# A two-layer decoder on one core: row of maxima ahead of maxima and values projection, stacked reciprocal parts, separate bank rings in the first attention

## What is computed

```python
# first attention: 16 heads of 8 numbers, softmax over 512 keys
dots = jnp.einsum('bhid,bhjd->bhij', q, k) * scale
attn = jax.nn.softmax(dots, axis=-1)
out = jnp.einsum('bhij,bhjd->bhid', attn, v)
# second attention: 16 heads of 64 numbers, queries from the 512 tokens,
# keys and values from 154 context rows and the same 512 tokens (666 keys)
w = jnp.einsum('bhqd,bhkd->bhqk', q * scale, k * scale)
w = jax.nn.softmax(w.astype(jnp.float32), axis=-1).astype(q.dtype)
out = jnp.einsum('bhqk,bhkd->bhqd', w, v)
return out.transpose(0, 2, 1, 3).reshape(B, S_lat, INNER) @ Wo
```

## Time and profile before

| what | value |
|---|---|
| median of 3 runs | 1617.49 us (1614.69 to 1625.23) |
| the profiled execution | 1627.39 us, its span 1625.6 us |
| mean granted TensorE clock | 0.973 |
| TensorE matmul busy | 1469.5 us, 90% |
| VectorE | 1122.3 us, 69% |
| ScalarE | 925.9 us, 57% |
| GpSimd | 695.2 us, 43% |
| chain that ended last | TensorE 61%, VectorE 17%, ScalarE 10%, issue 6%, GpSimd 4% |

### The profile page before, as it was taken

One profiled execution on the slowest core, in us unless ns is written; L12 is line 12 of the kernel. 1 busy time (PEld: TensorE's weight loads), 2 busy tenths in 40 slices (PEclk: granted clock), 3 DMA queues, 4 the chain that ended last, 5 costly groups with the idle time before them and its releaser, 6 DMA issues.

```text
span 1625.6 us, 44178 instructions
## 1 busy us (share of the span) xinstructions
PE 1469.5 (90%) x19224; PEld 802.6 (49%) x19224; DVE 1122.3 (69%) x2297; ACT 925.9 (57%) x1301; POOL 695.2 (43%) x736
## 2 busy tenths in 40 slices
PE   8888888899999999999987989799999989999996
PEld 4222222333335333433433545678777778775553
DVE  6677776888875785767555677666776765574664
ACT  2687776678876875777584333364556544342220
POOL 2111130566655665666483104468756667001010
PEclk9898999999999999999999999899999999989998
DMA  4000002333322232233120100000000001100000
GB/s 163 1 1 1 1 0 89 93 96 101 89 76 76 78 91 76 76 105 92 34 73 16 68 1 14 15 16 4 17 17 17 17 4 39 54 2 1 5 9 14
DMA packets 32417, 70.79 MB, mean 44 GB/s; under 512 B 5328, under 2 KB 7056, under 8 KB 31968
## 3 DMA queue, kind: packets, MB, share of 16 engines
q1 hardware_dynamic: 32224, 67.98, 14.3%
HBM read 47.45 MB, written 20.51 MB: 42 GB/s over the span
## 4 chain that ended last, share of the span: by engine, by line
PE 61%; DVE 17%; ACT 10%; issue 6%; POOL 4%; DMA 0%; ACTq 0%; DVEq 0%; POOLq 0%
PE ps L160 59%; DVE a_MX L432 4%; ACT b_X L957 3%; POOL b_EL L975 2%; ACT b_EH L169 2%; DVE b_mx L895 1%; PE ps L242 1%; POOL d_XI L1779 1%; POOL d_tmp L1776 1%; ACT b_Hk L169 1%; DVE b_rd L1067 1%; DVE b_VL L830 1%; DVE c_SG L1398 1%; DVE b_Lk L836 1%; DVE c_H L1404 1%
## 5 line engine op out<-in xcount | busy, mean ns | idle before, releaser
L975 POOL TENSOR_TENSOR b_EL<-b_X,b_EH 128x1024 f16<-128x1024 f32 x160 | 341.0, 2131 | 215.0 <-ACT b_EH L169 214.8
L957 ACT ACTIVATE b_X<-ps 128x1024 f32<-128x1024 f32 x160 | 163.7, 1023 | 108.2 <-PE ps L160 106.9
L1776 POOL TENSOR_TENSOR d_tmp<-d_G,d_XI 128x31 f32<-128x31 f32 (+15 forms) x248 | 126.6, 511 | 162.4 <-DVE d_G L1705 143.5
L432 DVE TENSOR_REDUCE a_MX<-ps 128x2 f16<-128x1024 f32 x128 | 155.3, 1227 | 57.2 <-PE ps L160 56.5
L895 DVE TENSOR_REDUCE b_mx<-ps 128x2 f32<-128x1024 f32 x128 | 156.0, 1219 | 55.7 <-PE ps L160 53.9
L169 ACT ACTIVATE b_EH<-b_X 128x1024 f16<-128x1024 f32 x160 | 169.1, 1057 | 25.5 <-PE ps L160 14.3
L160 PE MATMUL ps<-b_M,b_S 128*64 128x512 f16 (+1 forms) x1408 | 177.0, 383 | 3.1 <-ACT b_X L957 3.0
L469 ACT ACTIVATE a_E<-ps 128x1024 f32<-128x1024 f32 x128 | 131.1, 1024 | 58.3 <-PE ps L160 57.8
L1779 POOL TENSOR_TENSOR d_XI<-d_XI,d_tmp 128x31 f32<-128x31 f32 (+15 forms) x248 | 139.6, 563 | 19.4
L160 PEld LDWEIGHTS ps<-b_M,b_S 128*64 128x64 f16 (+1 forms) x1408 | 69.1, 108 | 86.5 <-issue 21.6
L451 POOL TENSOR_TENSOR a_QS<-a_QS,a_MR 128x512 f16<-128x512 f16 x16 | 18.5, 1156 | 213.8 <-ACT a_MR L169 209.6
(11 more groups left out here) (321 smaller groups left out, 3304.6 us busy)
## 6 DMA issues: line engine op xcount, KB each, us to landing
b_S<-s_xk SPq DMA_DIRECT2D x48, 336.0 KB, 6.4
b_M<-s_xq SPq DMA_DIRECT2D x48, 256.0 KB, 5.0
s_xk<-b_Hk SPq DMA_DIRECT2D x16, 336.0 KB, 2.2
s_xk<-b_Lk SPq DMA_DIRECT2D x16, 336.0 KB, 2.5
s_xq<-b_Hq SPq DMA_DIRECT2D x16, 256.0 KB, 2.0
s_xq<-b_Lq SPq DMA_DIRECT2D x16, 256.0 KB, 2.0
d_XI<-eye SPq DMA_DIRECT2D x8, 512.0 KB, 3.5
f_w<-f_w SPq DMA_DIRECT2D x1, 2048.0 KB, 8.4
```

The lines of the kernel that those rows point to most:

```text
L432: v.e.tensor_reduce(out, PS[:, bk:bk + 2, :], AX, ALU.max).then_inc(sem("a_mx"), 1)
L957: a.e.activation(b_X[k % 2], PS[:, bk:bk + 2, :], ACT.Exp, scale=0.125).then_inc(sem("b_ex"), 1)
L975: last = p.e.tensor_tensor(b_EL[k % 6], b_X[k % 2], b_EH[k % 6], ALU.subtract)
L1776: e.tensor_tensor(tm, a, x, ALU.mult).then_inc(*p.step())
```

## The change

1. `b_slot_tensor`: in slot 7 the order row, maxima, projection item, in place of item, maxima, row. Other slots are unchanged.
2. The two fp16 parts of the reciprocals are stacked in the partitions of one tile: `b_one` gets its ones a second time 16 columns on, so the sums stand twice in each 32 partitions; `b_rh` is the rounded value, and b_rp = b_rh * m + b_rd with m = 0 or -1 by partition (a fifth column of b_ln). `b_sel` has its entries in both places. A selection is then one product over 128 partitions, issued as two tiles of 64 columns, where it was two of 128 columns.
3. First attention: maxima, output products and key transposes take `ringQ` (banks 2 to 5), scores take `ringE` (banks 0 and 1).

```diff
+        ringQ, ringE = Ring(4, 2), Ring(2, 0)
...
         def a_max_tensor(t, G, s):
             hp, q, n = s // 4, s % 4, 8 * G + s
-            bk = ring.take(t, ("amx", n), 2, "a_mx", n + 1)
+            bk = ringQ.take(t, ("amx", n), 2, "a_mx", n + 1)
...
-            e, banks = t.e, ring if b < NB - 1 else aux
+            e, banks = t.e, ringQ if b < NB - 1 else aux
...
-            keys = b_keys_tensor(t, 0)
-            side = a_side(t, a_out_tensor, b_keys_tensor)
+            keys = b_keys_tensor(t, 0, ringQ)
+            side = a_side(t, a_out_tensor, lambda t, k: b_keys_tensor(t, k, ringQ))
...
-                        a_score_tensor(t, G, s, ring if p < NG else ringS)
+                        a_score_tensor(t, G, s, ringE)
...
-        b_rp = rB.take("b_rp", 512, F16).rearrange("p (k n) -> p k n", k=2)
+        b_rh = rB.take("b_rh", 256, F16)
+        b_rp = rB.take("b_rp", 256, F16)
...
-            e.memset(b_one[:, :, 0:4], 0.0).then_inc(*p.step())
+            e.memset(b_one[:, :, 0:4], 0.0)
+            e.memset(b_one[:, :, 16:20], 0.0).then_inc(*p.step())
             p.wait_own()
             for g in range(4):
-                last = e.memset(b_one[:, g, g:g + 1], 1.0 / SEL)
+                e.memset(b_one[:, g, g:g + 1], 1.0 / SEL)
+                last = e.memset(b_one[:, g, 16 + g:17 + g], 1.0 / SEL)
...
-                mm(e, PS[:, bk, :], b_sel[:, a, :], b_rp[:, 0, :], stop=False)
-                mm(e, PS[:, bk, :], b_sel[:, a, :], b_rp[:, 1, :], start=False).then_inc(sem("b_st"), 1)
+                for h in HALF:
+                    last = mm(e, PS[h, bk, :], b_sel[:, a, h], b_rp)
+                last.then_inc(sem("b_st"), 1)
...
-                e.tensor_copy(b_rp[:, 0, c], b_rd[:, c]).then_inc(*v.step())
+                e.tensor_copy(b_rh[:, c], b_rd[:, c]).then_inc(*v.step())
                 v.wait_own()
-                e.tensor_tensor(b_rp[:, 1, c], b_rd[:, c], b_rp[:, 0, c], ALU.subtract).then_inc(sem("b_rt"), 1)
+                stt(e, b_rp[:, c], b_rh[:, c], b_ln[:, 4:5], b_rd[:, c], ALU.mult, ALU.add).then_inc(sem("b_rt"), 1)
...
+            if s == 7:
+                if 0 <= u + 1 < NU:
+                    b_row_tensor(t, u + 1)
+                if mx:
+                    b_max_tensor(t, *mx)
             if b_item(x):
                 b_project_tensor(t, *b_item(x))
-            if mx:
+            if s != 7 and mx:
                 b_max_tensor(t, *mx)
...
-            if 0 <= u + 1 < NU and s == 7:
-                b_row_tensor(t, u + 1)
```

More of the change, by code:

```diff
@@ L657, in build @@
         b_wo = r0.take("b_wo", 1024).rearrange("p (a n) -> p a n", a=8)
-        b_ln = r0.take("b_ln", 4)
+        b_ln = r0.take("b_ln", 5)
         b_sel = r0.take("b_sel", 512, F16).rearrange("p (a n) -> p a n", a=8)
@@ L2719 @@
         heads[32 * (h % 4) + h // 4, h // 2, h % 2] = 1.0 / SEL
+        heads[32 * (h % 4) + 16 + h // 4, h // 2, h % 2] = 1.0 / SEL
     arrays |= {
@@ L2725 @@
         "x_wo": a["L0_xattn_Wo"].reshape(8, 128, D).transpose(1, 0, 2),
-        "x_ln": np.stack([a["L0_xattn_ln1_g"], a["L0_xattn_ln1_b"], a["L0_xattn_ln2_g"], a["L0_xattn_ln2_b"]], 1),
+        "x_ln": np.stack([a["L0_xattn_ln1_g"], a["L0_xattn_ln1_b"], a["L0_xattn_ln2_g"], a["L0_xattn_ln2_b"],
+                          np.where(np.arange(D) % 32 < 16, 0.0, -1.0).astype(np.float32)], 1),
         "c_sel": moe.reshape(48, 8, D),
```

## The result

| what | before | after |
|---|---|---|
| median of the runs | 1617.49 us (1614.69 to 1626.39, 5 runs) | 1601.5 us (1597.89 to 1602.48, 5 runs) |
| ratio after to before, 95% interval | | 0.9865 [0.9839, 0.9891] |
| the profiled execution, its span | 1627.39 us, 1625.6 us | 1597.89 us, 1596.1 us |
| mean granted TensorE clock of that execution | 0.973 | 0.981 |

The kernel became 1.35% faster, 16 us between the medians, where the prediction has 29.6 us and 1588 us. The means of these runs are 1620.1 and 1600.6 us, 19.5 apart.

A forecast was written before the change was run, and what follows sets the result against it. TensorE, 90% busy, was taken to bound the kernel, with waits mostly on VectorE. Terms -10 - 3.3 - 8.6 - 3.5 - 4.2 = -29.6 us, off the median 1617.5, gave 1588 us, range 1574 to 1609 us.

The forecast's parts named there:

- Slots 7 and 8, -10: Second attention: waits before the values products, 12.4 us, go except 2.4; saves 10 us, bounds -12.4 and 0.
- output product, -3.3: Second attention, between slots 7 and 8: three output products wait 0.4 to 0.6 us each for b_mrow; saves 3.3 us.
- less 16 units at 0.15 (2.4): Second attention, slot 7: loss of about 0.15 us per unit, the moved first values part waiting for b_Lk.
- So nothing is left to wait for: Second values part, slot 8: b_mrow is done at 570.57, before TensorE arrives at about 571.0.
- Stacked selection, -8.6: Second attention: 24 selections save 0.41 us each, 9.8 us, less 1.2 given back; bounds -9.8 and -3.8.
- Give back 1.2: Second attention: 1.2 us of the selections' saving lost because b_Lk ends one wait per batch and comes no sooner.
- First attention, -4.2: Separate score banks: 14 groups save 0.2 us each, 2.8, plus 1.4 of clock; bounds -25.4 and +8.
- Clock, -3.5: Clock falls at 294 to 302 and 494 to 500 us, following stalls, mostly or half go; bounds -7 and +3.
- rival 2: Clock stays up: falls in both stages and early ones go, 10 us more saved, 1578 us; chance 0.15.
- A saving of waits carries over unchanged: The 29.6 us saved against the profiled execution, 1627.4 us, also come off the runs' median, 1617.5, giving 1588 us.
- The wait only changes its name: Second attention: b_Lk comes late too and bank emptying eats the selection's gain; 1608 us, chance 0.15.
- Slower: First attention: one score bank pair ties TensorE to ScalarE and the clock falls each group; 1638 us, chance 0.04.

The follow-up runs named there:

- row_only: Changed kernel with slot 7 of the second attention in the order row, values projection, maxima: 1613.53 us, ratio 0.9930.
- only_order: Kernel before with only the new order of slot 7 (row, maxima, projection): 1611.91 us, ratio 0.9935.
- stack_full: Changed kernel with each selection as one product of 128 columns instead of two tiles of 64: 1604.76 us, ratio 0.9894.
- rings_swap: Changed kernel with two banks for the first attention's maxima, outputs and keys and four for the scores: 1639.42 us, ratio 1.0114.
- b_again: Kernel before, unchanged, run again as a kernel of its own: 1623.95 us, ratio 1.0014.
- only_rings: Kernel before with only the parted bank rings of the first attention: 1624.91 us, ratio 1.0015.
- rings_again: Kernel before with only the parted bank rings of the first attention, same program a second time: 1622.91 us.
- only_stack: Kernel before with only the stacked reciprocals: 1615.37 us, ratio 0.9961.
- a_again: Changed kernel, unedited, run again as a kernel of its own: 1606.89 us, ratio 0.9898.
- order_stack: Kernel before with slot 7's new order and the stacked reciprocals, without the new rings: 1612.3 us, ratio 0.9931.
- pv_first: Changed kernel with all values products and projections of the first attention issued ahead of their slot's scores: 1669.07 us, ratio 1.0274.
- balance: Changed kernel with three first-attention steps moved around the scores in slots 7, 0 and 1, none awaiting a_O's copy: 1609.57 us, ratio 0.9912.

## Why the prediction was right and wrong, point by point

**Direction and mechanism: right; the size too large (29.6 us against 16 between the medians and 20 between the means).** b_VL's wait is gone, the output product waits 0.36 us (forecast 0.5), values to scores take 0.43 (forecast 0.44), scores of the first attention wait for a_E with 0.95 in slot 7 (forecast 1.0), and the plain group is 13.34 us (forecast 13.3). The time lies in the range, 13.5 us above the forecast. For the group there is some luck in the sum: by the earlier trace rows a slot bound by ScalarE takes 0.47 + 1.02 + 0.05 = 1.54 us, not the 1.49 used, and in after five of the eight steps between exponentials, not four, last 1.51 to 1.53 us. The fifth replaces a slot priced at 1.63, and the two errors cancel.

**Slots 7 and 8, -10 and output product, -3.3: mis-sized.** Together they measured -8.5 over the fourteen units. The output products gave 3 x 1.32 = 4.0, so the slots gave about 4.5. The step that failed is "less 16 units at 0.15 (2.4)": I priced the wait at the moved projection and not the one at the moved maxima. row_only and only_order show both. The maxima left b_Lk with nothing to wait for (3.8 us in before and in only_order), and in exchange waited 3.3 us for b_mx; b_den and b_rp, VectorE's other results, added 2.4, all of it behind the three casts that fell beside GpSimd, which the prediction does not have. "So nothing is left to wait for" held for the one bank. The stretch holds 10.5 of the 12.4 us that the forecast started from; the other 1.9 lie before and behind it.

**Stacked selection, -8.6: right in mechanism, 2.3 too large.** The 0.41 per product was met by 15 of the 24; the other nine saved about 0.3, so "x24 = 9.8" was 9.0. "Give back 1.2" was the other short step: b_Lk and b_Lq took 2.3. With 0.4 that no row explains, -6.3 is left. The Trainium skill (TensorEngine Tiling (Array Packing), PSUM Bottleneck) says that emptying can become the bound. Here waits for emptying took 2.3 of the 9.0 us, a quarter and not the whole. The drain at a change of tiling mode (same page, Key Properties) agrees with 0.10 us at each boundary in stack_full and none at the plain selections of after.

**First attention, -4.2: right in its plain part.** 0.2 us per group as said, which the fit sees as -2.4 alone and -3.9 on top of the other two. Alone it moved no median. rings_swap shows that its worth depends on the four banks of the maxima.

**Clock, -3.5 and 1.4 of the term above: 2.5 in the means, about 10 in the profiled pair.** I took the falls of the profiled execution as consequences of the stalls just before them. In part they may be: at output products they came only behind the 1.68 us wait, 6 times in 15 with the old order and never in the 27 of the nine profiles with the new one. But the wait does not decide it: each kernel with the old order has it three times, with two falls in before and b_again, one in only_rings and rings_again, at different products, and none in only_stack. The fall at the start of the second attention is missing in after and a_again, but stands in full in only_order and stack_full, which have no wait for b_VL, so that stall does not decide this one. In the first attention the profiles are more even: four of the five without the new rings spend 24 us at the lower level there, order_stack 3, and the six with after's first attention 0 to 7. Within the profiled pair rival 2 ("the clock stays up") came about in part: 89 us at the lower level in before's execution and 62 in after's. Over the runs, before spent 72 us and after 66, so the clock gave 2.5 us where 4.9 were counted. Why the means do not follow the profiles is open.

**"A saving of waits carries over unchanged" to the median shown.** The waits did. The median of three, 1617.5, was itself low by 6 us against the mean of 85 runs, and the sum taken off it held 4.9 us of clock, which is no saving of waits.

**The account.** Forecast -29.6. Second attention 21.9 forecast, 13.7 measured: 8.2 short. Clock: 2.4 short. First attention 2.8 forecast, 3.9 measured: 1.1 better. Sum -20.1, and the means are 1623.3 and 1603.1, 20.2 apart. The 16 between the medians are less because before's median of five, 1617.5, lies 2.6 us below the mean of the same five and after's 0.9 above. The 29.5 us between the profiled executions hold, by the fit, the same 17.7 and a draw of the clock in after's favour (0.973 against 0.981, some 27 us at the lower level or 10 us of time); the 2 us left are within the scatter.

**The rivals.** "The wait only changes its name" was partly true, with other names: b_mx, b_den and b_rp, not b_Lk, took 5.7 of the 15.5 us. Its 1608 us lie nearer to the mean of after's ten runs, 1603.1, than my 1588 us. "The clock stays up" came about in part in the profiled executions, not in the mean. "Slower" was not this kernel, but pv_first shows its mechanism at its price.

## What to carry to other kernels

Where an engine at 90% stands still for many small waits on one other engine, removing one wait can give much less than it lasted (here 8.7 of 15.5 us), since that other engine's next result is late as well; count every result that TensorE now reaches earlier, not only the one whose bank was moved. Fill a wait with work only after asking what that work itself waits for, and look at the groups with side work as well as the plain one. Moving an engine's work in time can also bring it beside another engine's that it collides with. A profiled execution is one draw of the clock: take savings of clock from the mean over many runs, or leave them out.

## What the runs showed of the hardware that was not expected

**The clock falls differently in executions of the same work.** From 41 to 49 us the granted clock was 0.57 in b_again, 0.79 in order_stack and 1.00 in after, only_rings and row_only, which have the new rings, and 0.57 again in balance, which has the rings and another order. b_again and order_stack issue the same instructions there. So the same instructions can get another clock; only_rings and rings_again, one program, have their one fall at different output products. The draw is not free of the program, though: in this window all five profiles with the old rings lie below 1.00, and of the nine with parted rings only balance and rings_swap (0.75). The windows of b_again and order_stack, in this order:

```profile
41.00:49.00 8.00, 7.37 (x26) 1.75 (x26) 4.91 (x10) 4.14 (x5) 0.00 (x0) 0.57 0.01 3
```

```profile
41.00:49.00 8.00, 7.26 (x36) 2.16 (x36) 5.71 (x13) 5.79 (x8) 0.00 (x0) 0.79 0.01 3
```

Twelve runs of one kernel spread over 11 to 20 us, and the mean granted clock goes with most of that: 0.36 us per us at the lower level, with 1.6 us unexplained. At an output product the price is (9.04 - 7.41) / 3.4 = 0.48 (3.4 us at the lower level there, the 0.72 of 494 to 500 us in the earlier trace rows); I read the difference as waits that a slower TensorE covers elsewhere, which no run here tests.

**A small VectorE instruction beside GpSimd can take as long as GpSimd still needs.** VectorE's rounding of the reciprocals in after, its shortest, middle and longest duration in ns, and the long one in the timeline of VectorE and GpSimd:

```profile
L1078 DVE CAST b_rh<-b_rd x8: 281/290/1239, 440.1 to 847.0; 128x256 f16<-128x256 f32 x8
```

```profile
441.74 2.13 POOL L979 TENSOR_TENSOR b_EL<-b_X,b_EH 128x1024 f16<-128x1024 f32 x1 [1.73 <-ACT b_EH L169]
...
442.78 1.24 DVE L1078 CAST b_rh<-b_rd 128x256 f16<-128x256 f32 x1
444.06 0.48 DVE L172 SCALAR_TENSOR_TENSOR b_rp<-b_rh,b_ln,b_rd 128x256 f16<-128x256 f16 x1
...
444.69 0.41 PE L160 MATMUL ps<-b_rp,b_sel 128*64 128x512 f16 x2 [0.35 <-DVE b_rp L172]
```

GpSimd ends at 443.87, the cast at 444.02, and the first selection of the batch waits 0.35 us for b_rp behind both; b_den, which VectorE makes two results later, then costs TensorE 0.68 us (at 446.32). It is a pattern: of the eight casts of after the three that start inside a GpSimd instruction last 1.24 us and end 0.15 us after it, and the other five last 0.28 to 0.30. In before and only_stack no cast starts inside one, and none lasts longer than 0.30. The Trainium skill (SBUF — State Buffer, Who interferes with whom) says that VectorE and GpSimd share a pair of ports, that a cast can claim it, and that whoever comes second is blocked until the other's instruction ends; this trace agrees with it. Moving the cast away from GpSimd's instruction was not tried; it could win back up to the 3.2 us that after waits for b_rp and b_den in the fourteen units.
